# The last feed-forward rows of two tiles side by side, under another order of the steps

## What is computed

```
h = layernorm(x) * (1 + ca) + sa
x = x + ga * linear_attention(h)          # 16 heads of 16, causal running sums
h = layernorm(x) * (1 + cb) + sb
x = x + gb * layers(h)                    # two layers, DEPTH = 2
```

```
h = shift_token(x); q, k, v = split(h @ wqkv)          # 8 heads of 64
q, k = rotary(l2norm(q) * qs, l2norm(k) * ks)
x = x + local_attention(q, k, v) @ wo                  # windows of 128 tokens and the window before
h = layernorm(shift_token(x)) * lg + lb
a, g = split(h @ w1 + b1)                              # 682 hidden columns each
x = x + (a * gelu(g)) @ w2 + b2
```

## Time and profile before

| | |
|---|---|
| median of three runs | 3239.49 us |
| the profiled execution, its own time | 3241.86 us |
| span of its trace, first to last instruction | 3240.0 us |
| mean granted TensorE clock | 0.992 of full |
| TensorE busy (matmuls) | 3149.2 us, 97% |
| VectorE, GpSimd, ScalarE busy | 82%, 79%, 66% |
| DMA | 125.07 MB, mean 39 GB/s |
| attention phase | up to about 589 us |
| layers | from there to the end |

### The profile page before, as it was taken

How to read it: one execution, slowest core, us unless ns; L and a number is a source line. 1 busy time by engine, 2 the same in 40 slices (tenths; PEclk the granted TensorE clock), 3 DMA queues, 4 the chain that set the end, 5 groups by cost and what they waited for, 6 DMA issues and landing times.

```text
span 3240.0 us, 85044 instructions
## 1 busy us (share of the span) xinstructions
PE 3149.2 (97%) x25452; PEld 2440.9 (75%) x25452; DVE 2658.3 (82%) x8314; ACT 2144.6 (66%) x5372; POOL 2574.6 (79%) x2892
## 2 busy tenths in 40 slices
PE   6999999699999999999999999999999999999998
PEld 3777677477777777777777777777777777777777
DVE  5999999578777777777777788888888888888884
ACT  3666666367777776767677777776777676767674
POOL 3999999687777777777777778888888888888884
PEclk8999999899999999999999999999999999999999
DMA  7211111000000000000000001111111111111111
GB/s 234 64 48 48 47 50 45 27 22 24 24 25 24 25 24 25 24 24 25 24 24 25 24 25 37 37 37 38 37 38 37 38 37 37 38 37 37 38 37 30
DMA packets 148856, 125.07 MB, mean 39 GB/s; under 512 B 18356, under 2 KB 144808, under 8 KB 148144
## 3 DMA queue, kind: packets, MB, share of 16 engines
q1 hardware_dynamic: 141840, 108.56, 11.0%
q10 hardware_dynamic: 6560, 11.02, 1.1%
HBM read 77.49 MB, written 42.02 MB: 37 GB/s over the span
## 4 chain that ended last, share of the span: by engine, by line
PE 92%; POOL 3%; issue 2%; DVE 1%; ACT 1%; ACTq 0%; DMA 0%; DVEq 0%; POOLq 0%; SPq 0%
PE bank L559 33%; PE bank L760 19%; PE bank L768 10%; PE bank L566 9%; PE bank L733 7%; PE bank L712 6%; PE bank L627 2%; PE bank L645 2%; POOL shared L1303 1%; PE bank L607 1%; PE bank L610 1%; PE bank L638 1%; PE bank L656 1%; PE bank L746 0%; PE bank L675 0%
## 5 line engine op out<-in xcount | busy, mean ns | idle before, releaser
L760 PEld LDWEIGHTS bank<-zT,W 128*128 128x128 f32 x5632 | 667.2, 192 | 137.5 <-issue 135.1
L559 PE MATMUL bank<-WQKV,xT 128*128 128x512 f32 x1536 | 744.3, 607 | 11.2 <-ACT xT L784 6.5
L1339 POOL TENSOR_TENSOR rnorm<-clamped,HALF 128x8 f32<-128x8 f32 x256 | 420.4, 1642 | 411.9 <-DVE clamped L1168 405.4
L760 PE MATMUL bank<-zT,W 128*128 128x128 f32 x5632 | 671.0, 275 | 14.0 <-issue 12.0
L1352 POOL TENSOR_TENSOR shared<-shared,share_of 128x512 f32<-128x512 f32 x512 | 585.6, 1171 | 59.0 <-DVE shared L1203 59.0
L934 ACT ACTIVATE shared<-shared,negmax 128x256 f32<-128x256 f32 x1024 | 505.6, 495 | 26.8 <-DVE negmax L1187 25.2
L559 PEld LDWEIGHTS bank<-WQKV,xT 128*128 128x128 f32 x1536 | 263.4, 191 | 221.8 <-issue 214.0
L1165 DVE TENSOR_REDUCE sums<-rotary_work 128x8 f32<-128x512 f32 x256 | 175.6, 686 | 285.3 <-ACT rotary_work L904 281.0
L1203 DVE COPY_PREDICATED shared<-BEYOND,shared 128x256 f32<-128x256 int32 x512 | 399.2, 791 | 0.0
L1187 DVE CUSTOM_DVE_ANT_0 shared<-bank,MASK 128x256 f32<-128x256 f32 x1024 | 366.2, 420 | 0.1
L1362 POOL TENSOR_TENSOR shared<-shared,IDENT 128x256 f32<-128x256 f32 x512 | 362.1, 728 | 0.0
(11 more groups left out here) (157 smaller groups left out, 6649.7 us busy)
## 6 DMA issues: line engine op xcount, KB each, us to landing
X<-xl_rows SPq DMA_DIRECT2D x128, 128.0 KB, 2.1
X<-in_x SPq DMA_DIRECT2D x64, 128.0 KB, 2.1
x_tiles<-ax SPq DMA_DIRECT2D x64, 128.0 KB, 1.7
xl_rows<-axl SPq DMA_DIRECT2D x64, 128.0 KB, 1.7
XS<-xl_rows SPq DMA_DIRECT2D x128, 64.0 KB, 2.1
xm_rows<-X SPq DMA_DIRECT2D x128, 64.0 KB, 1.6
xs<-xm_rows SPq DMA_DIRECT2D x128, 64.0 KB, 1.8
xl_rows<-X SPq DMA_DIRECT2D x64, 128.0 KB, 1.7
```

The lines of the kernel that those rows point to most:

```text
L559: mm = nc.tensor.matmul(held(tile, key)[:, 0:cols], lhsT[c], rhs[c], start=(c == 0), stop=(c == len(lhsT) - 1))
L760: mm = nc.tensor.matmul(held(tile, key)[:, k * P:(k + 1) * P], W1[:, tile.l, c, at:at + P], zT[:, c], start=(c == 0), stop=(c == KC - 1))
L1339: G.tensor_tensor(rnorm[q][:], clamped[q][:], HALF[:].to_broadcast((P, LH)), ALU.pow).then_inc(done[f"root_{key}"], 1)
```

## The change

It has two parts.

*Tails side by side.* The left-over rows of an even tile now go to partitions 0 to 41 of `hid_tail`, those of an odd tile to partitions 64 to 105. w2's last 42 rows are loaded twice, at partitions 0 and 64, so there is one more load for each layer. narrow sums only the five full matmuls and signals `narrowed`. In the narrow step of the odd tile, two matmuls with 64 contraction rows follow, one on the lower and one on the upper half, each finishing the sum in its own tile's bank; they signal `filled["nw"]` twice. The gates wait for `narrowed` of the tile before, and the last one also for the sums of two tiles before; add_f does nothing for an even tile and adds both tiles for an odd one. So in two slots two full-array matmuls (two passes each) become two on half of the array's rows; all other instructions stay.

*Another order.* `ORDER_L` is replaced: the deepest TensorE step has depth 4; project_v, age_k, keep_k, keep_v have depth 1, square_q 0, project_o and add_o 2, turn_z, norm, root_x, add_b2, affine 3, widen0 3, and widen1, widen2, gelu, gates, narrow, add_f 4; finish and store stay at 5. `BANK_L` and `BANK_A` (not shown) are new; `ORDER_A` stays.

```diff
--- before.py
+++ after.py
@@ -61,33 +61,33 @@
            (3, "a_mask1")],
 }
 ORDER_L = {
-    "SP": [(0, "load"), (3, "shift"), (3, "late"), (5, "store")],
-    "PE": [(5, "widen0"), (5, "widen1"), (3, "project_o"), (2, "turn_p1"), (0, "turn_x"), (2, "turn_p0"), (1, "turn_q"),
-           (0, "project_k"), (5, "narrow"), (4, "turn_z_first"), (1, "ready_score"), (4, "turn_z_last"), (1, "score"),
-           (2, "weigh0"), (2, "weigh1"), (2, "weigh2"), (2, "weigh3"), (0, "project_v"), (4, "widen2"), (0, "turn_k"),
-           (0, "project_q")],
-    "ACT": [(1, "square_q"), (0, "age_k"), (4, "norm"), (5, "gelu"), (0, "keep_x"), (1, "keep_q"), (0, "square_k"),
-           (4, "affine"), (1, "exp0"), (1, "exp1"), (1, "exp2"), (1, "exp3"), (0, "keep_k"), (0, "keep_v"), (2, "keep_o")],
-    "DVE": [(1, "sum_q"), (1, "rotate_q"), (5, "gate0"), (5, "gate1"), (3, "add_o"), (5, "gate2"), (2, "keep_p0"),
-           (2, "keep_p1"), (0, "sum_k"), (0, "rotate_k"), (3, "stats"), (5, "add_f"), (1, "max0"), (1, "max1"), (1, "max2"),
-           (1, "max3"), (1, "invert0"), (1, "invert1"), (1, "invert2"), (1, "invert3")],
-    "POOL": [(2, "share3"), (2, "diagonal0"), (1, "root_q"), (1, "scale_q"), (2, "diagonal1"), (2, "diagonal2"),
-           (2, "diagonal3"), (4, "add_b2"), (0, "root_k"), (0, "add_k"), (0, "scale_k"), (3, "root_x"), (5, "finish"),
-           (1, "share0"), (1, "share1"), (1, "share2")],
+    "SP": [(0, "load"), (3, "shift"), (4, "late"), (5, "store")],
+    "PE": [(4, "widen1"), (4, "widen2"), (2, "turn_p0"), (1, "project_v"), (1, "turn_q"), (0, "turn_x"), (4, "narrow"),
+           (2, "turn_p1"), (0, "project_k"), (3, "turn_z_first"), (1, "ready_score"), (3, "turn_z_last"), (1, "score"),
+           (2, "weigh0"), (2, "weigh1"), (2, "weigh2"), (2, "weigh3"), (3, "widen0"), (2, "project_o"), (0, "project_q"),
+           (0, "turn_k")],
+    "ACT": [(1, "age_k"), (1, "keep_k"), (4, "gelu"), (1, "keep_v"), (0, "keep_x"), (1, "keep_q"), (3, "norm"),
+           (0, "square_k"), (3, "affine"), (2, "keep_o"), (1, "exp0"), (1, "exp1"), (1, "exp2"), (1, "exp3"), (0, "square_q")],
+    "DVE": [(1, "sum_q"), (1, "rotate_q"), (4, "gate0"), (4, "gate1"), (4, "gate2"), (3, "stats"), (2, "keep_p0"),
+           (4, "add_f"), (2, "keep_p1"), (0, "sum_k"), (0, "rotate_k"), (1, "max0"), (1, "max1"), (1, "max2"), (1, "max3"),
+           (1, "invert0"), (1, "invert1"), (1, "invert2"), (2, "add_o"), (1, "invert3")],
+    "POOL": [(2, "share2"), (1, "root_q"), (1, "scale_q"), (2, "share3"), (2, "diagonal0"), (2, "diagonal1"), (2, "diagonal2"),
+           (2, "diagonal3"), (3, "root_x"), (3, "add_b2"), (5, "finish"), (0, "root_k"), (0, "add_k"), (0, "scale_k"),
+           (1, "share0"), (1, "share1")],
 }
...
 BANK_L = {
-    "ag0": "47404747", "ag1": "30616215", "wo": "06215253", "p1": "62153030", "x": "47474747", "p0": "06215353",
-    "qT": "21530626", "k": "74747474", "nw": "30606215", "z": "62151530", "sim0": "15306212", "sim1": "74747474",
-    "sim2": "21530626", "sim3": "30621535", "o": "62153430", "v": "74747475", "ag2": "62171530", "kT": "06215306",
-    "q": "21530623",
+    "ag1": "06010205", "ag2": "42351437", "p0": "56611725", "v": "01030403", "qT": "17324534", "x": "57621576",
+    "nw": "73246341", "p1": "25566172", "k": "04070205", "o": "30403010", "z": "23546371", "sim3": "16314735",
+    "sim2": "57621574", "sim1": "35463122", "sim0": "62157647", "ag0": "53646321", "wo": "02050507", "q": "74275264",
+    "kT": "16314737",
 }
...
@@ -317,7 +317,7 @@
             sem("silu_ready"), sem("gate_step"), sem("modrow_full"), sem("modrow_ready"))
         consts_ready, factors_ready, rows_moved = sem("consts_ready"), sem("factors_ready"), sem("rows_moved")
 
-        WEIGHT_LOADS, LAYER_LOADS = 7, 12 * DEPTH + 6
+        WEIGHT_LOADS, LAYER_LOADS = 7, 13 * DEPTH + 6
         ROWS_STORED = 2 * DEPTH + 1
         NCONST = 8 + 2 * DEPTH
 
@@ -764,10 +764,16 @@
             def narrow(tile):
                 after(pe, done["gate"], tile)
                 claim(pe, tile, "nw")
-                for m in range(HC):
-                    mm = nc.tensor.matmul(held(tile, "nw")[:, 0:D], hid[:, m] if m < HC - 1 else hid_tail[:], W2[:, tile.l, m],
-                                          start=(m == 0), stop=(m == HC - 1))
-                mm.then_inc(filled["nw"], 1)
+                for m in range(HC - 1):
+                    mm = nc.tensor.matmul(held(tile, "nw")[:, 0:D], hid[:, m], W2[:, tile.l, m], start=(m == 0), stop=False,
+                                          skip_group_check=True)
+                mm.then_inc(done["narrowed"], 1)
+                if tile.s % 2 == 1:
+                    for s in (tile.s - 1, tile.s):
+                        rows = slice(s % 2 * LD, s % 2 * LD + LD)
+                        mm = nc.tensor.matmul(bank[int(BANK_L["nw"][s])][:, 0:D], hid_tail[rows], W2[rows, tile.l, HC - 1],
+                                              start=False, stop=True, skip_group_check=True)
+                    mm.then_inc(filled["nw"], 2)
 
             steps = {"turn_x": turn_x, "turn_q": turn_q, "turn_k": turn_k, "project_o": project_o, "turn_z": turn_z, "narrow": narrow}
             steps.update({f"project_{k}": partial(project_qkv, k) for k in "qkv"})
@@ -814,7 +820,8 @@
                     load(W1[:, l, :, g * FULL:(g + 1) * FULL], chunks[:, :, 0:FULL])
                     load(W1[:, l, :, 2 * FULL + g * LD:2 * FULL + g * LD + LAST], chunks[:, :, FULL:])
                 load(W2[:, l, 0:HC - 1], w2[l, 0:FULL].rearrange("(c p) n -> p c n", p=P))
-                load(W2[0:LAST, l, HC - 1], w2[l, FULL:HID])
+                for e in range(2):
+                    load(W2[e * LD:e * LD + LAST, l, HC - 1], w2[l, FULL:HID])
                 load(B1G[LD:LD + LAST, l:l + 1], b1[0:LAST, (2 * l + 2) * HC - 1:(2 * l + 2) * HC])
             load(B2[:], broadcast(b2))
             load(B1[:], b1)
@@ -1234,22 +1241,28 @@
 
             def gate(m, tile):
                 after(dve, done[f"gelu{m}"], tile)
-                after(dve, filled["nw"], tile, back=1)
+                after(dve, done["narrowed"], tile, back=1)
+                if m == HC // 2 - 1:
+                    after(dve, filled["nw"], tile, back=2)
                 first_use(dve, tile)
+                tail = tile.s % 2 * LD
                 for k in (2 * m, 2 * m + 1):
                     rows = LAST if k == HC - 1 else P
                     b = (tile.l * 2) * HC + k
                     at = 2 * (k % 2) * P
-                    to = hid[:, k] if k < HC - 1 else hid_tail[0:LAST]
+                    to = hid[:, k] if k < HC - 1 else hid_tail[tail:tail + LAST]
                     ins = V.scalar_tensor_tensor(out=to, in0=held(tile, f"ag{m}")[0:rows, at:at + P],
                                                  scalar=B1[0:rows, b:b + 1], in1=gl[0:rows, k], op0=ALU.add, op1=ALU.mult)
                 if f"gate{m}" == latest(ORDER_L["DVE"], ["gate0", "gate1", "gate2"]):
                     ins.then_inc(done["gate"], 1)
 
             def add_f(tile):
+                if tile.s % 2 == 0:
+                    return
                 after(dve, filled["nw"], tile)
                 after(dve, done["add_b2"], tile)
-                V.tensor_tensor(X[tile.s][:], X[tile.s][:], held(tile, "nw")[:, 0:D], ALU.add).then_inc(done["add_f"], 1)
+                for s in (tile.s - 1, tile.s):
+                    V.tensor_tensor(X[s][:], X[s][:], bank[int(BANK_L["nw"][s])][:, 0:D], ALU.add).then_inc(done["add_f"], 1)
 
             steps = {"rotate_q": partial(rotate, 0), "rotate_k": partial(rotate, 1), "sum_q": partial(square_sums, 0), "sum_k": partial(square_sums, 1),
                      "add_o": add_o, "stats": stats, "add_f": add_f}
```

More of the change, by code:

```diff
@@ L111 @@
              "add_q", "summed_q", "sum_q", "max0", "max1", "max2", "max3", "invert0", "invert1", "invert2", "invert3", "add_o",
-             "stats", "norm", "gate", "add_f", "add_k", "root_k", "scale_k", "root_q", "scale_q", "share0",
+             "stats", "norm", "gate", "narrowed", "add_f", "add_k", "root_k", "scale_k", "root_q", "scale_q", "share0",
              "share1", "share2", "share3", "root_x", "add_b2", "gated", "finish", "weigh0", "weigh1", "weigh2", "weigh3", "other_mask",
```

6 lines of the change are left out of this document (3 added, 3 removed).

## The result

The changed kernel takes 3381.53 us (median of four runs, 3380.22 to 3386.86) where the kernel before takes 3240.74 beside it: a ratio of 1.044, 95% interval 1.0427 to 1.0453. It is 141 us slower, and 125 above the forecast of 3256.

A forecast was written before the change was run, and what follows sets the result against it. TensorE was taken to bound the kernel at 20.12 us a slot. The new ring's waits, with the tails' 4.5 us saving included, add 31 us; the ends take off 14: +17 on 3239.5 gives 3256, range 3215 to 3288.

The forecast's parts named there:

- second rival: VectorE's masked copies wait for whole GpSimd shares: ring 21.4 us in all slots, 3383 us; chance with blocked q addition 0.08.
- 0.3 for invert3's masked copy and the clamp: VectorE's wait-prone steps beside GpSimd's shares, ahead of sum_q: 0.3 us, bounds 0 and 1.2.
- the ring: Chain from one weigh step to the next over ScalarE, VectorE, GpSimd and TensorE: 20.26 us, bounds about 19.7 and 21.1.
- The argument against the collision: VectorE starts invert2's copy as its last step ends; GpSimd's share1 needs a 0.1 us hand-over first, so the copy leads.
- the q addition: VectorE step beside GpSimd's root: 0.69 us, not slowed, nothing added; if blocked, ring 20.8 and 3310 us, chance 0.02.
- the even slots: Layer slots with 19.69 us of TensorE work; TensorE waits 0.57 us at the first turn of z.
- scale_q ends at 10.9 us ... and TensorE is at turn_q at 11.15 ... I cost them at nothing: Times counted from the weigh: scale_q is done before TensorE turns q; thin, but costed at nothing.
- The branch of the loop at every eighth slot stays.: Loop branch after every eight layer slots: taken as staying, with no cost added.
- The tightest claim (sim0 after p1) has 0.4 us: Bank claim of sim0 after p1: 0.4 us to spare, costed at nothing, bound 0.4 us a slot.
- The tails: Left-over rows in narrow: 0.79 us a pair against 0.86, 64 pairs save 4.5 us; slots hold 19.69 and 20.48.
- up to 2x: Skill's promise for 64-row contractions: 0.43 us a pair, 27.5 us in all; free change of form had chance 0.02.
- The ends: Filling and emptying the layers with one step less: gain 7.5 at the start, 6.5 at the end, together 14 us.

The follow-up runs named there:

- the copy always first: Changed kernel with each invert's masked copy on VectorE put ahead of its reciprocal instead of behind it; 3301.19 us, ratio 1.0188.
- root_x early alone: Changed kernel with root_x on GpSimd moved from behind the four diagonals to behind the first; 3370.01 us, ratio 1.0408.
- Moving the cut alone: Changed kernel with the loop's branch placed ahead of sum_k on VectorE and ahead of the norm on ScalarE; 3284.73 us, ratio 1.0139.
- 3291.04: Changed kernel with old left-over rows, invert3 behind sum_q, root_x behind diagonal0, branch ahead of keep_p0 (VectorE) and norm (ScalarE); 3291.04 us, ratio 1.0171.
- 3233.94: The 3291.04 kernel with another BANK_L, in which every claim has 1 us to spare; 3233.94 us, ratio 0.9988.
- the single run: Kernel before with side-by-side tails alone, own order, another bank table, finish, late and store one or two slots later; 3235.40 us, ratio 0.9992.

## Why the prediction was wrong

The result is beside my second rival's 3383, to which I gave 0.06, and outside my range. The mechanism is the rival's; that the number fits so well is luck: the rival had every slot at 21.4 and the branches at nothing, while in fact 69% of the normal slots are that long and the branches make up for the rest.

**The term that failed** is "0.3 for invert3's masked copy and the clamp" in the ring, with bounds of 0 and 1.2. It is 0.11 in a short slot (the sum at 4.69 us from the first exponential, where eight of them and square_q give 4.58) and 1.23 in a long one. My upper bound of 1.2 had room for that; the range of the forecast, which ended at 3288, left it out. The argument against the collision, that VectorE goes on at once while GpSimd needs a hand-over of 0.1, was wrong at the decisive place: invert2's copy stands behind a reciprocal that takes 0.08 from start to start, so the two come within 40 ns of each other. I should have seen that my two estimates, 0.1 against VectorE's own steps, could not tell an order of starts apart, and given the case far more than 0.06. The Trainium skill (SBUF — State Buffer, Who interferes with whom) says: "Issue order, not op shape, decides who blocks." I used that section for the q addition alone. The trace agrees with the sentence: 1.31 and 1.04 us, or 0.44 and 1.34.

**The rest of the ring was right, its sum with some luck.** With the copy always first (3301.19), the even slots are 20.22 (forecast 20.26), the odd ones 20.52 (20.48), the mean 20.41 (20.37), with waits ahead of the two turns of z, 0.29 and 0.20 us in the even slots, and none at the turn of q. Four terms are off and cancel: in an even slot TensorE's hand-over to ScalarE takes 0.11 (0.2), square_q to sum_q with copy and clamp 0.75 (0.93), the norm until the turn of z 0.93 (1.10), and the way from the turn of z to the end of the weigh steps 3.90 (3.57), of which 0.20 is the second turn's wait. The account of this kernel closes: its slots cost 34 us over the kernel before, the branches 35 and the ends give 8, 61 in all, where the spans differ by 61.7.

**"scale_q ends at 10.9 us ... and TensorE is at turn_q at 11.15 ... I cost them at nothing".** That held only while nothing in front of it slipped. With the long copy, scale_q slips by 1.12, and the turn of q closes a second ring. This is why root_x early alone gave 11 us instead of 140.

**"The branch of the loop at every eighth slot stays."** It was the second largest error, 38 us. In the order before, VectorE's restart fell on a wait: VectorE waits 2.29 us for ScalarE at that place in a slot without a branch, and 3.3 to 4.1 us at the 12 branches. In the new one the sum of squares, first behind the branch, is on the ring. Moving the cut alone took that away (3284.73), and part of the long copies with it, for a reason that stays open.

**"The tightest claim (sim0 after p1) has 0.4 us".** Right for the changed kernel, where it doesn't wait. But it is what holds as soon as root_x is moved, and without the tails a table exists that is free of it (3291.04 to 3233.94). The tails hold a bank for a slot longer, and I take that for their price, rather than TensorE's time. No other table was tried with them in this order, so that they must cost this is not shown.

**The tails** were right to 0.01 us a slot: 19.69 and 20.48, and no more than 5 us for the whole. Of the up to 2x that the Trainium skill (TensorEngine Tiling (Array Packing), Theoretical Speedup) names, by my estimate 27.5 us here, the single run shows 3, with an interval that touches none.

**The ends** gave 12.9 us for a forecast of 14, though split otherwise: 4.9 at the start (7.5) and 8.0 at the end (6.5). The q addition wasn't slowed, as I took it: 0.69.

## What to carry to other kernels

Where a step of VectorE and one of GpSimd are released by the same event, work out which starts first, and if your estimates can't tell the two starts apart (here they were 0.04 us apart), count both cases; then make one of them certain with an instruction's place, as the copy ahead of its reciprocal does. When an order leaves no slack in a ring, look for the second ring just behind it, and ask where the loop's branch cuts each engine's order: it belongs where that engine waits anyway. A result kept in PSUM for a slot longer has a price in the other claims.

## What the runs showed of the hardware

- A masked copy with its operands in SBUF and a GpSimd multiplication exclude each other for a whole instruction (1.31 and 1.04 us, or 0.44 and 1.34); the order is decided by a few nanoseconds (in the changed kernel all copies are short up to 32 ns behind, and all are long from 35 ns). A copy that starts 0.04 to 0.09 us ahead of the root over 8 columns makes the root 1.80 to 1.86 us long for 1.65. The q addition, which starts 1.1 to 1.5 us into the root, takes 0.69 us in all 127 cases and isn't slowed.
- One program runs in two regimes side by side, slots of 20.46 and 21.36 us. With the branch at another place of the order 32 of the 94 normal slots are of the long kind, for 65.
- Behind a taken branch VectorE stood 2.2 to 5.4 us without an instruction, 3.7 at the one shown. Behind the 2.9 us that TensorE waited for it there, TensorE's granted clock was 0.66 of full, and its ten passes took 3.85 us for 2.32. Such slow passes stood behind 8 of the 12 branches, after waits of 2.0 to 4.2 us, and not behind the other 4, after waits of 2.2 to 2.4.
